# The order of weighing and scanning on VectorE in the last stage of a vision-tower kernel

## The chip, the cores and the metric

The kernel runs on one core of a Trainium2 chip. The metric is the device time of one execution in microseconds (us). A core has TensorE (PE), VectorE (DVE), ScalarE (ACT), GpSimd (POOL) and SyncE (SP). They run their own instruction streams in order and meet only at semaphores.

## What is computed

A tokenizer (two attention blocks over image patches), then one layer: a state-space scan and a mixture of experts. The program has three stages; only the third, which holds the scan and the experts, is touched. Its scan is this part of the reference, with 16 states (N) for each of 768 channels (D), 4 images, 3136 tokens:

```python
delta = jax.nn.softplus(x @ W_D + b_D + p_Delta)
dA = delta[..., None] * A
A_bar = jnp.exp(dA)
B_bar = (A_bar - A) / dA * delta[..., None] * Bproj[:, :, None, :]

def step(h, inp):
    a, b, c, xl = inp
    h = a * h + b * xl[..., None]
    y = jnp.einsum('bn,bdn->bd', c, h)
    return (h, y)
```

## The kernel before

The third stage is the function `tail`. Tokens are cut into 28 units of 448 (UNITS, T). A unit has 24 steps (STEPS); a step k takes 128 channels times four of the 16 states, laid out as four groups g = 0 to 3 of 128 rows and 448 tokens. Groups 0 and 1 are the first pair, 2 and 3 the second. `n` is the running number of a step, 672 in all. For each step:

- POOL `weigh_in` (L1622) writes x times B into a slot of the ring `v`, six slots; two steps later `weigh_out` (L1634) multiplies the scanned slot by C.
- ACT `step` (L1928) writes the decays, exp(A times delta), of a pair into PSUM (`decay(g)`), two instructions a pair. Each pair has one PSUM place, so the decays of a pair for step k wait until the scan of that pair for step k-1 is done (`free_pair`).
- DVE `weigh` (L2038) turns a group of the slot into (decay - A) times v. It waits for both decays of its pair, by the semaphore `s_a`.
- DVE `scan` (L2047) runs the recurrence over both groups of a pair at once, 901 elements long. It waits for the weighings of its pair (`s_wt`), and for the first pair also for the start states, which ACT writes (`start_states`, L1899).
- ACT `keep_states` (L1889) copies the last states of all four groups when both scans are done. POOL's `weigh_out` waits for it.
- PE `step` (L1734) sums over the states after POOL's `weigh_out`.

ACT's order within step k is: start states of k, decays of the first pair of k, then other work due at k, then the states kept of k-1, then decays of the second pair of k, then other work due at k + 0.5. The other work belongs to the neighbouring units: projection, normalisation and delta of the unit ahead (`front`), the experts of the unit behind (`mlp`). Constants such as A_GL = 17 or V_OH = 13 say at which step it stands. Step 17 holds most of ACT's: two table loads, four Gelu (L1952), three Relu (L1873). On DVE the other work stands behind step k: L2090 (one expert product, at 12, 14, 15 and 16), L2121 (the mask, two at 17 and two at 18), L2028 (delta, at 18 and 19) and small ones. PE makes the products that L2090 and L2121 take (L1665, L1785).

OWN is empty, so `own_scan` is never taken.

Of the kernel before, what the change touches and what calls it, by code (L numbers as in the profile page):

```python
# [1281 lines left out]
OWN = ()  # L1282
# [4 lines left out]
def others(n):  # L1287

    i, k = divmod(n, STEPS)
    return i * (STEPS - len(OWN)) + sum(j not in OWN for j in range(k + 1))  # L1290

def owned(n):

    return n + 1 - others(n)

def tail(nc, sem, w, c, t2, w1c, xd, dd, bcd, out):

    with ExitStack() as ctx:  # L1300
# [10 lines left out]
        def decay(g):  # L1311

            at = g // 2 * 1024 + g % 2 * GW
            return flat[:, at + 2:at + T + 2]

        def decays(pair):
            row = flat[:, 1024 * pair:1024 * pair + 2 * GW]
            return row.rearrange("p (g t) -> p g t", g=2)[:, :, 2:T + 2]
# [685 lines left out]
        def _(dve):  # L2004
# [26 lines left out]
            def weigh(i, k, g):  # L2031

                n = STEPS * i + k
                if g == 0:
                    dve.wait_ge(s_v, n + 1)
                dve.wait_ge(s_a, 4 * n + g // 2 * 2 + 2)
                row = v[:, n % RING, g, 2:T + 2]
                stt(row, decay(g), aa[:, 4 * k + g:4 * k + g + 1], row, ALU.subtract, ALU.mult).then_inc(s_wt, 1)  # L2038

            def scan(i, k, pair):  # L2040

                n = STEPS * i + k
                row = v[:, n % RING, 2 * pair:2 * pair + 2, :].rearrange("p g t -> p (g t)")[:, 1:GW + T + 2]
                if pair == 0:
                    dve.wait_ge(s_s0, others(n))
                dve.wait_ge(s_wt, 4 * n + 2 * pair + 2)
                nc.vector.tensor_tensor_scan(row, flat[:, 1024 * pair + 1:1024 * pair + GW + T + 2], row, 0.0, ALU.mult,  # L2047
                                             ALU.add).then_inc(s_sc, 1)

            def own_scan(i, k, pair):  # L2050

                n = STEPS * i + k
                first = i % J3 == 0
                if not first:
                    dve.wait_ge(s_sv, 2 * owned(n - STEPS) + pair - 1)
                for g in range(2 * pair, 2 * pair + 2):
                    dve.wait_ge(s_wt, 4 * n + g + 1)
                    nc.vector.tensor_tensor_scan(decay(g), decay(g), v[:, n % RING, g, 2:T + 2],
                                                 0.0 if first else st[:, 4 * k + g:4 * k + g + 1], ALU.mult,
                                                 ALU.add).then_inc(s_sp, 1)  # L2060
                if k // Q == 0 and pair == 0:
                    dve.wait_ge(s_lc[k % Q], 16 * (i + 1))
                dve.wait_ge(s_sp, 4 * owned(n) + 2 * pair - 2)
                tt(v[:, n % RING, 2 * pair:2 * pair + 2, 2:T + 2], decays(pair),
                   ct[:, k % Q:k % Q + 1, :].to_broadcast([128, 2, T]), ALU.mult).then_inc(s_cv, 1)

            def step(i, k):
                for pair in range(2):
                    weigh(i, k, 2 * pair)
                    weigh(i, k, 2 * pair + 1)  # L2070
                    if k in OWN:
                        own_scan(i, k, pair)
                    else:
                        scan(i, k, pair)

            def mlp(i, k):
                if k == V_VAR:
# [80 lines left out]
            for i in range(UNITS + 1):  # L2158
                for k in range(TAIL if i == UNITS else STEPS):
                    if i < UNITS:  # L2160
                        step(i, k)
                    if i >= 2 and k + STEPS < TAIL:
                        mlp(i - 2, k + STEPS)
                    if i >= 1:
                        mlp(i - 1, k)
                    if i + 1 < UNITS:
                        front(i + 1, k)
# [156 lines left out]
```

## Time and profile before

| | us |
|---|---|
| median of 3 runs | 8267.98 |
| lowest, highest | 8265.39, 8268.63 |
| the profiled execution | 8263.06 |
| its span on the core | 8261.3 |
| of it from the first L2038 to the last scan | 4935 |

The span is what the trace covers; the 1.8 us around it are launch and end. The profiled execution stands 4.9 us below the median. The page gives the busy time of each engine, the trace single instructions with the idle time ahead of each and what ended it.

### The profile page before, as it was taken

To read this page: it belongs to the slowest core of one execution; us is meant where nothing else is said; L and a number is where in the kernel's file an instruction comes from. 1 tells how busy PE (TensorE), PEld (TensorE's weight loads), DVE (VectorE), ACT (ScalarE), POOL (GpSimd) and SP (SyncE) were. 2 spreads that over 40 slices of the span, in tenths; PEclk is the share of its full clock that TensorE was granted. 3 is DMA by queue.
4 is the path that set the end of the run, shared out by engine and by line. 5 is a ranking of instruction groups with operands and counts; after the bars stand their busy time and mean duration, and the time that the engine had idled before them with its cause. 6 is when DMAs were issued, how large, how long until landed. Compare 5 with 4: busy or idle time off the path is not lost.

```text
span 8261.3 us, 86870 instructions
## 1 busy us (share of the span) xinstructions
PE 7327.8 (89%) x31004; PEld 2931.6 (35%) x31004; DVE 6205.4 (75%) x6573; ACT 4337.3 (53%) x7781; POOL 5547.7 (67%) x2487
## 2 busy tenths in 40 slices
PE   8999999869999975688888888888888888888987
PEld 6444444324444421133333333333333333333323
DVE  2566666742333345999999999999999999999995
ACT  3666666753444433555555555555555555555552
POOL 0111111148766614989999889999889998889994
PEclk9999999989999987789999889998989998988988
DMA  1111111135554413233333333333333333333331
GB/s 40 34 47 42 46 43 38 45 77 114 102 103 100 102 34 107 93 124 120 120 110 116 114 124 120 120 110 116 111 128 120 120 110 116 110 126 122 121 107 54
DMA packets 358648, 786.32 MB, mean 95 GB/s; under 512 B 72229, under 2 KB 284726, under 8 KB 350728
## 3 DMA queue, kind: packets, MB, share of 16 engines
q1 hardware_dynamic: 322168, 690.47, 28.4%
q0 software_dynamic: 21712, 51.75, 2.5%
q10 hardware_dynamic: 14336, 38.54, 1.3%
q8 instruction: 246, 4.03, 0.2%
q14 instruction: 186, 1.52, 0.1%
HBM read 597.06 MB, written 183.35 MB: 94 GB/s over the span
## 4 chain that ended last, share of the span: by engine, by line
DVE 28%; PE 15%; issue 11%; POOL 4%; ACT 4%; DMA 0%; DVEq 0%; SPq 0%; ACTq 0%; POOLq 0%
DVE v L2038 13%; DVE v L2047 13%; PE ps L1665 3%; POOL v L1634 3%; PE ps L1670 2%; PE ps L1672 2%; PE ps L1734 2%; PE ps L1679 2%; POOL v L1622 1%; DVE dl L2028 1%; PE ps L1681 1%; PE ps L1785 1%; ACT ps L1928 1%; ACT gm L1952 1%; PE ps L1798 0%
## 5 line engine op out<-in xcount | busy, mean ns | idle before, releaser
L2047 DVE TENSOR_TENSOR_SCAN v<-ps,v 128x901 f32<-128x901 f32 x1344 | 2732.1, 2033 | 95.0 <-DVE v L2038 2.7
L1634 POOL TENSOR_TENSOR v<-v,ct 128x1792 f32<-128x1792 f32 x672 | 2257.6, 3360 | 479.0 <-ACT st L1889 477.8
L1622 POOL TENSOR_TENSOR v<-xr,bt 128x1792 f32<-128x1792 f32 x672 | 2258.1, 3360 | 82.3 <-DMA xr<-h_by_channel 82.3
L1928 ACT ACTIVATE ps<-dr,aa 128x448 f32<-128x448 f32 x2688 | 1595.9, 626 | 1319.6 <-DVE v L2047 1303.2
L2038 DVE SCALAR_TENSOR_TENSOR v<-ps,aa,v 128x448 f32<-128x448 f32 x2688 | 1687.5, 669 | 71.5 <-ACT ps L1928 67.9
L1734 PE MATMUL ps<-v,dg 128*32 128x448 f32 x5376 | 792.3, 632 | 616.2 <-POOL v L1634 395.1
L236 POOL DMA_DIRECT2D tokens<-ob x448 | 235.3, 532 | 1529.9 <-DVE ob L563 1486.9
L1798 PE MATMUL ps<-w_or_w,gm 128*112 128x384 f32 x1792 | 694.4, 535 | 3.0 <-DMA w_or_w<-in_w 3.0
L1665 PE MATMUL ps<-h,w_or_w 128*128 128x448 f32 x1344 | 588.7, 592 | 84.9 <-DVE bcs L2022 84.9
L1889 ACT ACTIVATE st<-v 128x4 f32<-128x4 f32 x672 | 140.9, 210 | 893.5 <-DVE v L2047 893.5
L1670 PE MATMUL ps<-x,wpa 128*128 128x448 f32 x1008 | 497.1, 632 | 7.6 <-DVE w_or_w L2154 6.9
L1734 PEld LDWEIGHTS ps<-v,dg 128*32 128x32 f32 x5376 | 126.3, 114 | 1026.3 <-POOL v L1634 550.2
L1798 PEld LDWEIGHTS ps<-w_or_w,gm 128*112 128x112 f32 x1792 | 338.6, 197 | 386.9 <-issue 174.4
L1672 PE MATMUL ps<-x,wpb 64*128 64x448 f32 x1008 | 452.2, 580 | 0.0
L929 PE MATMUL ps<-xt,wa 128*64 128x448 f32 x2016 | 435.1, 565 | 0.0
L552 DVE COPY ht<-ps 112x512 f32<-112x512 f32 x112 | 77.4, 691 | 464.8 <-ACT kp L433 464.8
L1665 PEld LDWEIGHTS ps<-h,w_or_w 128*128 128x128 f32 x1344 | 268.4, 206 | 408.3 <-issue 302.6
L586 DVE RECIPROCAL qpn<-qpn 128x448 f32<-128x448 f32 x112 | 330.7, 2953 | 3.9
L1238 DVE TENSOR_TENSOR kq<-ps,rsa 128x896 f32<-128x896 f32 x56 | 61.1, 1091 | 358.4 <-PE ps L937 337.5
L1670 PEld LDWEIGHTS ps<-x,wpa 128*128 128x128 f32 x1008 | 202.0, 210 | 260.3 <-issue 257.8
L290 PE MATMUL ps<-wki,h 128*112 128x256 f32 x896 | 275.9, 389 | 1.9 <-DVE hu L544 1.9
L1672 PEld LDWEIGHTS ps<-x,wpb 64*128 64x128 f32 x1008 | 175.8, 187 | 275.1 <-issue 275.1
(328 smaller groups left out, 11558.6 us busy)
## 6 DMA issues: line engine op xcount, KB each, us to landing
xr<-h_by_channel SPq DMA_DIRECT2D x168, 896.0 KB, 4.9
dr<-delta_by_channel SPq DMA_DIRECT2D x168, 896.0 KB, 4.7
x<-tokens SPq DMA_DIRECT2D x252, 224.0 KB, 5.3
tokens<-ob POOLq DMA_DIRECT2D x448, 112.0 KB, 2.4
w_or_w<-in_w SPq DMA_DIRECT2D x29, 1536.0 KB, 6.4
w_or_w<-centred_w SPq DMA_DIRECT2D x27, 1536.0 KB, 9.0
h_by_channel<-h SPq DMA_DIRECT2D x112, 336.0 KB, 4.8
delta_by_channel<-dl SPq DMA_DIRECT2D x224, 168.0 KB, 2.8
```

Source lines behind the costliest of these rows:

```text
L586: nc.vector.reciprocal(qpn[:, u % 3, :], qpn[:, u % 3, :]).then_inc(s_dr, 1)
L929: mm(ps[half[g], o, 0:T], wa[:, j, cols], xt[:, 2 * (n % 3) + g, 0:TR2, j:j + 2 * S2 - 1:2], start=(j == 0), stop=False)
L1622: tt(v[:, n % RING, :, 2:T + 2], xr[:, dc % 2, :].rearrange("p (i t) -> p i t", i=4), bt[:, q:q + 1, :].to_broadcast([128, 4, T]), ALU.mul ...
L1634: tt(v[:, n % RING, :, 2:T + 2], v[:, n % RING, :, 2:T + 2], ct[:, q:q + 1, :].to_broadcast([128, 4, T]), ALU.mult).then_inc(s_cm, 1)
L1665: last = mm(into, weights(dc), h[:, i % 3, dc, :], start=(dc == 0), stop=(dc == DC - 1))
L1670: mm(into, even(j), x3[:, 0:TR3, j:j + 2 * S3 - 1:2], start=(j == 0), stop=False)
L1672: return mm(into, odd(j - 3), x3[0:64, 1:TR3 + 1, j - 3:j - 4 + 2 * S3:2], start=False, stop=(j == 5))
L1734: last = mm(ps[32 * g:32 * g + 32, YB, 0:T], dg[:, 4 * k + g, :], v[:, n % RING, g, 2:T + 2], start=(q == 0), stop=False)
L1798: mm(into[:, 0:D // 2], gm[:, m, cs], w2[:, m, lo:lo + D // 2], start=(m == 0), stop=False)
L1928: fn(decay(g), dr[:, dc % 2, g, :], ACT.Exp, scale=aa[:, 4 * k + g:4 * k + g + 1]).then_inc(s_a, 1)
L2038: stt(row, decay(g), aa[:, 4 * k + g:4 * k + g + 1], row, ALU.subtract, ALU.mult).then_inc(s_wt, 1)
L2047: nc.vector.tensor_tensor_scan(row, flat[:, 1024 * pair + 1:1024 * pair + GW + T + 2], row, 0.0, ALU.mult, ALU.add).then_inc(s_sc, 1)
```

## The change

On DVE, `step` weighs groups 0, 1 and 2, scans the first pair, weighs group 3 and scans the second pair. Before it weighed 0 and 1, scanned, weighed 2 and 3, and scanned. The instructions are the same ones, and each keeps its waits. The branch to `own_scan` goes, and with OWN empty nothing goes with it. Behind the edit line numbers fall by two (L2090 and L2121 become L2088 and L2119).

```diff
             def step(i, k):
-                for pair in range(2):
-                    weigh(i, k, 2 * pair)
-                    weigh(i, k, 2 * pair + 1)
-                    if k in OWN:
-                        own_scan(i, k, pair)
-                    else:
-                        scan(i, k, pair)
+                for g in range(3):
+                    weigh(i, k, g)
+                scan(i, k, 0)
+                weigh(i, k, 3)
+                scan(i, k, 1)
```

DVE around step 17 (from the last L2090 to the first L2028), before. The scan prints as SCALAR_TENSOR_TENSOR with 901 elements.

```order
L2090 TENSOR_TENSOR gm<-ps,rs2t 128x448
L2038 SCALAR_TENSOR_TENSOR v<-ps,aa,v 128x448 x2
L2047 SCALAR_TENSOR_TENSOR v<-ps,v 128x901
L2038 SCALAR_TENSOR_TENSOR v<-ps,aa,v 128x448 x2
L2047 SCALAR_TENSOR_TENSOR v<-ps,v 128x901
L2121 TENSOR_TENSOR gm<-gm,ps 128x448 x2
```

The same place in the changed kernel:

```order
L2088 TENSOR_TENSOR gm<-ps,rs2t 128x448
L2038 SCALAR_TENSOR_TENSOR v<-ps,aa,v 128x448 x3
L2047 SCALAR_TENSOR_TENSOR v<-ps,v 128x901
L2038 SCALAR_TENSOR_TENSOR v<-ps,aa,v 128x448
L2047 SCALAR_TENSOR_TENSOR v<-ps,v 128x901
L2119 TENSOR_TENSOR gm<-gm,ps 128x448 x2
```

The third weighing stands ahead of the first scan, in this step as in all 672. The other engines' streams are the same in both. ACT around step 17, from the decays of the first pair of step 17 to the decays of the second pair of step 18:

```order
L1928 ACTIVATE ps<-dr,aa 128x448 x2
L1952 ACT_TABLE_LOAD
L1952 ACTIVATE gm<-gm,b 128x448 x4
L1953 ACT_TABLE_LOAD
L1873 ACTIVATE dl<-ps,pc 128x448 x3
L1889 ACTIVATE st<-v 128x4
L1928 ACTIVATE ps<-dr,aa 128x448 x2
L1873 ACTIVATE dl<-ps,pc 128x448 x3
L1899 ACTIVATE v<-st 128x4
L1928 ACTIVATE ps<-dr,aa 128x448 x2
L1917 ACTIVATE h<-ps 128x448
L1878 ACTIVATE dl<-dl,small 128x1344
```

The second L1928 here holds the decays for which the third and fourth weighings of step 17 wait, the third L1928 those of the first pair of step 18, which follow the first scan of step 17.

## Rows read from the trace of the kernel before

**Rows 1.** Stretches: us, then each engine's busy us (and instructions), clock, DMA.

```profile
3221.00:8156.00 4935.00, 4237.14 (x15031) 1557.72 (x15032) 4674.94 (x4815) 2615.80 (x5542) 4457.14 (x1341) 0.89 0.35 115
```

**Rows 2.** Groups by line, 5600 to 7200: busy us, mean ns; idle before, releasers.

```profile
L2047 DVE TENSOR_TENSOR_SCAN v<-ps,v 128x901 f32<-128x901 f32 x434 | 882.2, 2033 | 30.8 <-ACT v L1899 0.9 <-DVE v L2038 0.5
L2038 DVE SCALAR_TENSOR_TENSOR v<-ps,aa,v 128x448 f32<-128x448 f32 x867 | 544.4, 669 | 19.0 <-ACT ps L1928 17.8
L1928 ACT ACTIVATE ps<-dr,aa 128x448 f32<-128x448 f32 x868 | 515.4, 626 | 425.1 <-DVE v L2047 425.1
```

**Rows 3.** Timeline, DVE, a step without other work: start us, us, instruction.

```profile
6020.90 1.25 DVE L2038 SCALAR_TENSOR_TENSOR v<-ps,aa,v 128x448 f32<-128x448 f32 x2
6022.25 2.03 DVE L2047 TENSOR_TENSOR_SCAN v<-ps,v 128x901 f32<-128x901 f32 x1
6024.20 1.25 DVE L2038 SCALAR_TENSOR_TENSOR v<-ps,aa,v 128x448 f32<-128x448 f32 x2
6025.49 2.03 DVE L2047 TENSOR_TENSOR_SCAN v<-ps,v 128x901 f32<-128x901 f32 x1
6027.44 1.25 DVE L2038 SCALAR_TENSOR_TENSOR v<-ps,aa,v 128x448 f32<-128x448 f32 x2
```

**Rows 4.** Timeline, ACT, the same step.

```profile
6021.02 0.21 ACT L1889 ACTIVATE st<-v 128x4 f32<-128x4 f32 x1 [2.04 <-DVE v L2047]
6021.13 1.18 ACT L1928 ACTIVATE ps<-dr,aa 128x448 f32<-128x448 f32 x2
...
6024.32 1.20 ACT L1928 ACTIVATE ps<-dr,aa 128x448 f32<-128x448 f32 x2 [1.88 <-DVE v L2047]
```

**Rows 5.** Timeline, ACT, step 1 of a unit.

```profile
6045.44 1.50 ACT L1843 ACTIVATE sq<-h 128x448 f32<-128x448 f32 x3
6047.17 0.21 ACT L1889 ACTIVATE st<-v 128x4 f32<-128x4 f32 x1 [0.23 <-DVE v L2047]
```

**Rows 6.** Timeline, DVE, other work ahead of step 8, step 12 and step 15.

```profile
6092.95 0.62 DVE L2079 TENSOR_TENSOR rs2t<-ps,rs2t 32x448 f32<-32x448 f32 x1
...
6121.13 1.26 DVE L2038 SCALAR_TENSOR_TENSOR v<-ps,aa,v 128x448 f32<-128x448 f32 x2
...
6143.66 0.62 DVE L2090 TENSOR_TENSOR gm<-ps,rs2t 128x448 f32<-128x448 f32 x1 [0.53 <-PE ps L1665]
```

**Rows 7.** Timeline, ACT, the decays of the second pair of step 12.

```profile
6121.96 1.20 ACT L1928 ACTIVATE ps<-dr,aa 128x448 f32<-128x448 f32 x2
```

**Rows 8.** Timeline, all engines, steps 17 and 18.

```profile
6164.52 0.21 ACT L1889 ACTIVATE st<-v 128x4 f32<-128x4 f32 x1
6164.62 1.20 ACT L1928 ACTIVATE ps<-dr,aa 128x448 f32<-128x448 f32 x2
6164.81 3.36 POOL L1634 TENSOR_TENSOR v<-v,ct 128x1792 f32<-128x1792 f32 x1 [6.97 <-ACT st L1889]
...
6165.85 1.28 DVE L2038 SCALAR_TENSOR_TENSOR v<-ps,aa,v 128x448 f32<-128x448 f32 x2 [2.03 <-ACT ps L1928]
...
6168.50 0.56 ACT L1917 ACTIVATE h<-ps 128x448 f32<-128x448 f32 x1
6168.92 1.44 ACT L1878 ACTIVATE dl<-dl,small 128x1344 f32<-128x1344 f32 x1
...
6170.24 0.22 ACT L1889 ACTIVATE st<-v 128x4 f32<-128x4 f32 x1
...
6171.45 3.36 POOL L1634 TENSOR_TENSOR v<-v,ct 128x1792 f32<-128x1792 f32 x1
...
6174.86 1.72 PE L1734 MATMUL ps<-v,dg 128*32 128x448 f32 x8 [4.03 <-POOL v L1634]
...
6178.48 0.62 DVE L2121 TENSOR_TENSOR gm<-gm,ps 128x448 f32<-128x448 f32 x1 [1.69 <-PE ps L1785]
```

**Rows 9.** Waits of DVE from 3400 on: us in total, times, longest.

```profile
DVE gm L2121 <- PE ps L1785: 70.1, 58, 2.0
...
DVE gm L2090 <- PE ps L1665: 48.6, 51, 5.6
```

## The prediction

> **What bounds the kernel now.** I read the stretches first. From the first weighing to the last scan DVE is busy for 4675 of 4935 us, 95%; POOL 90%, PE 86%, ACT 53% [rows 1]. So in this stage DVE sets the pace, and time added to its chain is time added to the kernel unless a wait of DVE swallows it. The groups by line say what it does: scans of 2.03 us and weighings of 0.67 [rows 2]. ACT's decays show 425 us of idle time ahead of them, all ended by DVE's scans: ACT is quick but lives on what DVE frees. So a loop runs through both: scan, decays, weighing, scan. The question is how much slack that loop has, and the timeline of a plain step answers it.
>
> **A plain step before** [rows 3]. With the first weighing's start as 0, the first scan starts at 1.35, the third weighing 1.95 later (3.30), the second scan at 4.59, the next step at 6.54. Two weighings span 1.25 us at 0.67 each, so the second starts 0.58 behind the first: neighbours without a wait between them overlap. The scan starts only behind the end of the weighing it needs: 0.10 after it for the first pair (1.35 against 1.25), 0.04 for the second (1.29 against 1.25).
>
> The decays of the second pair [rows 4]: the previous second scan ends, ACT keeps the states at 6021.02, starts the two decays at 6021.13 and is done at 6022.31, 1.41 after the first weighing of the step. DVE sees that 0.03 later (6164.62 + 1.20 = 6165.82, weighing at 6165.85 [rows 8]), so they are usable at **1.44**. The old third weighing came at 3.30: slack 1.86.
>
> **The same step after.** Nothing is added or removed; one weighing moves ahead of one scan. It would start at 2 x 0.58 = 1.16, and has to wait until 1.44: a new wait of 0.28. Queued behind it on DVE are both scans and the fourth weighing, and behind the first scan ACT's next decays. From there: scan 0.60 behind it (1.28 for two at 6165.85, after an idle moment, less 0.67 is 0.61 [rows 8]; 0.58 otherwise), at 2.04. Its own inputs were done at 1.25, so the bubble ahead of this scan goes. Fourth weighing 1.95 later, 3.99. It alone takes about 0.66, the second scan starts 0.04 behind: 4.69. Next step 6.64. So a plain step goes from 6.54 to 6.64, **+0.10**.
>
> Where the decays are early enough, the step is 1.16 + 0.58 + 1.95 + 0.70 + 1.95 = 6.34, **-0.20**. That is so where DVE has other work between the second scan and the next first weighing (0.62 us in L2079, say [rows 6]), which gives ACT the 0.28.
>
> Neither price is in the trace, since no third weighing stands ahead of a scan. Bounds: the follow-on of the scan behind an unrelated instruction is between 0.50 and 0.67, and the single weighing with its scan between 0.66 and 0.74; that makes a plain step +0.0 to +0.2.
>
> **One unit of 24 steps**, added up:
>
> - 13 plain steps (0 to 7, 9, 11, 21 to 23): 13 x 0.10 = +1.3.
> - Step 1. ACT's other work there leaves 0.23 us before it keeps the states [rows 5]. From first to second scan DVE now takes 1.95 + 0.70 = 2.65 in place of 1.95 + 1.29 = 3.24, 0.59 less, so ACT is late by 0.59 - 0.23: +0.36. At the other plain steps ACT has 0.85 or more there and hides it.
> - Step 12. The decays are done at 6121.96 + 1.20 = 6123.16 and usable at 6123.19 [rows 7]; the third weighing would start at 6121.13 + 1.16 = 6122.29 [rows 6]. Wait 0.90, less the 0.20: +0.7. The old order hid it behind the first scan.
> - Steps 8, 10, 15, 19, 20 have cover: 5 x -0.20 = -1.0.
> - Steps 13 and 14 have cover too, but L2090 behind step 14 waits 0.53 us for PE now [rows 6], and PE's products follow POOL, which follows the scans of step 12. The 0.4 won becomes a longer wait: 0.
> - Steps 16 to 18. The first scan of step 16 comes 0.40 later within its step (0.58 for the weighing put ahead of it, less the bubble of 0.18). ACT's decays for step 17 wait for it, then the table loads, Gelu and Relu, then the states kept and the second decays: all +0.40, and the DVE wait of 2.03 at 6165.85 with them [rows 8]. At that place the new order has a whole scan more behind the wait, some 1.9 us that used to lie in front. Is it on the path? What ends last there is the chain by which the mask product reaches L2121: states kept of step 17, POOL L1634 at 6171.45, PE at 6174.86, L2121 at 6178.48, before which DVE idles 1.69 [rows 8]. After, without the 0.40: first scan 6166.45 to 6168.48, decays of step 18 to 6169.65, L1917 and L1878 (0.42 and 1.32 from start to next start) to 6171.4, states kept then, POOL 0.29 later at 6171.7 in place of 6171.45. DVE itself gets to L2121 at about 6178.5. So +0.25, and with the 0.40 **+0.65**; 1.2 us of the 1.9 go into the old wait. The gain of step 16 is lost, since the chain leaves from its first scan.
>
> Sum: 1.3 + 0.36 + 0.7 - 1.0 + 0 + 0.65 = **+2.0 us a unit**, 28 units: +56 us. The profiled execution would go from 8263 to 8319, the median from 8268 to **8324**.
>
> SyncE, POOL and PE issue the same streams; no DMA moves. POOL needs 2 x 3.36 = 6.72 a step, more than a plain step of 6.54, but made up for at each unit's waits; a slower DVE only eases that.
>
> The trace shows that DVE neighbours overlap unless one waits for the other (1.25 for two weighings of 0.67 [rows 3]), which is what the new order uses. 
>
> **The rivals.**
>
> 1. *The bubble stays* (that rule as a mechanism): the scan starts as far behind the unrelated third weighing as it did behind its own second. Then covered steps gain nothing, plain ones lose the full 0.28: 13 x 0.28 + 0.36 + 0.9 + 0.65 = 5.5 a unit, +155, 8423. Against: 1.25 is less than 2 x 0.67, and scan to weighing is 1.95 at a length of 2.03 [rows 3]. Chance 0.05.
> 2. *Step 17 is exposed.* The scan behind the Gelu wait lands on the path: +1.95 in place of 0.65, 1.3 x 28 = +36, 8360. It decides at L2121: my working has DVE arrive only 0.2 us ahead of PE. Chance 0.15.
> 3. *The old waits swallow it.* DVE waits for PE 70.1 + 48.6 us in this stage [rows 9], 4 us a unit, twice what I add. If PE's products came at times of their own, the delay would vanish: 8268 to 8285. Against: PE waits for POOL, and POOL for states kept behind the scans, so they move along. Chance 0.13.
> 4. *Faster: the bubble outweighs the wait.* The price of a plain step is the wait less 0.18; the unit breaks even at 2.0 / 13 = 0.15 below my +0.10, at a wait of 0.13 us in place of 0.28. With no wait at all it is 13 x -0.20 for 13 x 0.10, -1.9 a unit, 8215. For: 0.28 is a difference of numbers near 1.4. Against: it begins with the end of the previous scan and ACT's order is fixed. Chance 0.07.
>
> **How the numbers follow.** My forecast has 0.60. 0.2% is 16.5 us, about what a measurement of this kernel can tell from no change. Slower: forecast, rivals 1 and 2, 0.80. Same: rival 3, 0.13. Faster: rival 4, 0.07. Range: 8324 with +-0.07 for a plain step is +-25; rival 2 takes the top to 8365; the upper part of rival 3 the bottom to 8278. Rivals 1, 4 and half of 3 stay outside, 0.19.
>
> **What would show it.** Plain steps of 6.64 us, with L2038 in a form of three, then one, and an idle time of some 0.3 us inside the three, released by ACT L1928; in all L2038 should wait for it some 13 x 0.28 x 28 = 100 us more from plain steps, 25 from step 12, 10 from step 1. No idle time ahead of the first scan. The wait of L2121 for PE falls from 1.69 to about 0.5 at its first. The 2.03 ahead of the third weighing of step 17 becomes about 4. I am wrong if plain steps measure under 6.5 or over 6.75, or if L2121's waits don't shrink.

## The result

| us | before | changed |
|---|---|---|
| median of 5 runs | 8267.98 | 8299.93 |
| lowest, highest | 8265.39, 8271.39 | 8298.85, 8301.81 |
| span of the profiled execution | 8261.3 | 8298.1 |

The changed kernel takes 1.0039 times as long, 95% interval 1.0024 to 1.0054. That is 32 us more; the prediction was 56 us more, 8324, with a range of 8278 to 8365, and "slower" at 0.80. The direction, the mechanism and most prices held. The sum was 24 us too high.

The stage's stretch, answering [rows 1] (us; then PE, PE loads, DVE, ACT, POOL busy us and instructions; clock; DMA share; GB/s), and the groups by line, answering [rows 2]:

```profile
3223.00:8191.00 4968.00, 4230.90 (x15027) 1551.32 (x15028) 4649.46 (x4815) 2623.37 (x5542) 4461.68 (x1341) 0.89 0.35 114
```

```profile
L2047 DVE TENSOR_TENSOR_SCAN v<-ps,v 128x901 f32<-128x901 f32 x432 | 876.1, 2028 | 7.5
L2038 DVE SCALAR_TENSOR_TENSOR v<-ps,aa,v 128x448 f32<-128x448 f32 x863 | 554.2, 671 | 73.7 <-ACT ps L1928 72.5
L1928 ACT ACTIVATE ps<-dr,aa 128x448 f32<-128x448 f32 x864 | 512.9, 625 | 533.1 <-DVE v L2047 532.9
```

The stage is 33 us longer, while DVE's busy time fell by 25 us. The idle time ahead of the scans went from 30.8 to 7.5 us in these 1600 us: that is the bubble. The idle time ahead of the weighings went from 19.0 to 73.7, nearly all of it ended by ACT's decays: that is the new wait. Both things that the change does are in these two differences, and the second, 55 us, is larger than the first, 23 us. Some 23 of the 55 us are no loss, though: these 1600 us hold nine units, and in each the wait at step 17 grew by 2.5 us, most of which the waits for the mask products gave back, as the rows of steps 17 and 18 below show.

A plain step of DVE in the changed kernel, from the timeline, answering [rows 3]:

```profile
6062.82 1.25 DVE L2038 SCALAR_TENSOR_TENSOR v<-ps,aa,v 128x448 f32<-128x448 f32 x2
6064.26 0.68 DVE L2038 SCALAR_TENSOR_TENSOR v<-ps,aa,v 128x448 f32<-128x448 f32 x1 [0.19 <-ACT ps L1928]
6064.86 2.02 DVE L2047 TENSOR_TENSOR_SCAN v<-ps,v 128x901 f32<-128x901 f32 x1
6066.80 0.66 DVE L2038 SCALAR_TENSOR_TENSOR v<-ps,aa,v 128x448 f32<-128x448 f32 x1
6067.50 2.03 DVE L2047 TENSOR_TENSOR_SCAN v<-ps,v 128x901 f32<-128x901 f32 x1
6069.45 1.25 DVE L2038 SCALAR_TENSOR_TENSOR v<-ps,aa,v 128x448 f32<-128x448 f32 x2
```

From 6062.82 the third weighing starts at 1.44, the first scan at 2.04, the fourth weighing at 3.98, the second scan at 4.68, the next step at 6.63. The prediction had 1.44, 2.04, 3.99, 4.69 and 6.64. The wait reads 0.19 and not 0.28 because the profile counts idle time from the end of the second weighing (0.67 long), and the third would have started 0.09 before that end.

ACT around the same step, answering [rows 4]:

```profile
6062.94 0.21 ACT L1889 ACTIVATE st<-v 128x4 f32<-128x4 f32 x1 [0.98 <-DVE v L2047]
6063.05 1.18 ACT L1928 ACTIVATE ps<-dr,aa 128x448 f32<-128x448 f32 x2
...
6066.92 1.19 ACT L1928 ACTIVATE ps<-dr,aa 128x448 f32<-128x448 f32 x2 [2.56 <-DVE v L2047]
```

The decays of the second pair end at 6064.23 and the weighing starts at 6064.26. ACT starts the copy as soon as the previous scan is done. So this step is a closed loop without slack: second scan, copy, decays, third weighing, first scan, fourth weighing, second scan.

Steps 17 and 18, answering [rows 8], all engines:

```profile
6188.56 1.20 ACT L1928 ACTIVATE ps<-dr,aa 128x448 f32<-128x448 f32 x2
...
6189.79 0.68 DVE L2038 SCALAR_TENSOR_TENSOR v<-ps,aa,v 128x448 f32<-128x448 f32 x1 [4.75 <-ACT ps L1928]
...
6195.62 3.36 POOL L1634 TENSOR_TENSOR v<-v,ct 128x1792 f32<-128x1792 f32 x1 [0.17 <-ACT st L1889]
...
6199.03 1.72 PE L1734 MATMUL ps<-v,dg 128*32 128x448 f32 x8 [3.15 <-POOL v L1634]
...
6202.64 0.62 DVE L2119 TENSOR_TENSOR gm<-gm,ps 128x448 f32<-128x448 f32 x1 [0.18 <-PE ps L1785]
```

DVE idles 4.75 us ahead of the third weighing of step 17, where it idled 2.03 (the prediction had about 4), and 0.18 us ahead of the third mask product, where it idled 1.69. So the scan that now stands behind the long wait goes mostly into the old wait, as worked out.

DVE's waits from 3400 on, answering [rows 9]:

```profile
DVE v L2038 <- ACT ps L1928: 214.2, 404, 4.8
DVE gm L2088 <- PE ps L1665: 51.6, 39, 5.9
DVE gm L2119 <- PE ps L1785: 28.6, 55, 0.9
```

The wait for the decays was 51.5 us before, all of it at step 17. Now step 17 has 120 us of it, the 12 plain steps other than step 1 have 62, step 12 has 21 and step 1 has 11. The prediction had 100, 25 and 10 for the last three; the 100 is too high because it counts 0.28 a step where the profile, as above, shows 0.19.

**The ledger.** The trace gives the start of each first weighing, so the length of each of the 24 steps. The table has the mean over the 26 units between the first and the last, changed kernel less before, beside the prediction, in us a unit:

| steps | predicted | measured |
|---|---|---|
| 0 to 7, 9, 11, 21 to 23 (step 1 among them) | +1.66 | +1.36 |
| 8, 10, 15, 19, 20 | -1.0 | -1.03 |
| 12 | +0.7 | +0.38 |
| 13, 14 | 0 | -0.05 |
| 16 to 18 | +0.65 | +0.53 |
| sum | +2.0 | +1.19 |

1.19 x 28 is 33 us. Of the +0.38 at step 12, 0.13 is one single wait of 3.3 us in the second unit, ahead of L2088 for a product of TensorE; no other unit of this trace has one over 0.2 us there.

### The profile page after: what moved, and what is told of

Its sections match the earlier page's. It is cut to its first block, busy times and chain, and to the rows that moved or that the text cites. A ratio compares the mean times of both kernels' runs of the same rounds, so it can differ in the third digit from the quotient of the medians.

```text
span 8298.1 us, 86870 instructions
## 1 busy us (share of the span) xinstructions
PE 7325.2 (88%) x31004; PEld 2926.6 (35%) x31004; DVE 6180.9 (74%) x6573; ACT 4345.5 (52%) x7781; POOL 5552.9 (67%) x2487
## 4 chain that ended last, share of the span: by engine, by line
DVE 30%; PE 11%; ACT 9%; issue 8%; POOL 4%; DMA 0%; SPq 0%; DVEq 0%; ACTq 0%; POOLq 0%
DVE v L2047 21%; ACT ps L1928 6%; DVE v L2038 5%; POOL v L1634 3%; PE ps L1665 2%; PE ps L1672 2%; POOL v L1622 1%; PE ps L1679 1%; DVE dl L2028 1%; PE ps L1734 1%; PE ps L1785 1%; PE ps L1670 1%; PE ps L1681 1%; ACT gm L1952 1%; PE ps L1798 1%
## 5 line engine op out<-in xcount | busy, mean ns | idle before, releaser
L1928 ACT ACTIVATE ps<-dr,aa 128x448 f32<-128x448 f32 x2688 | 1595.6, 625 | 1677.7 <-DVE v L2047 1660.8
L2038 DVE SCALAR_TENSOR_TENSOR v<-ps,aa,v 128x448 f32<-128x448 f32 x2688 | 1726.2, 671 | 238.1 <-ACT ps L1928 234.5
L1798 PE MATMUL ps<-w_or_w,gm 128*112 128x384 f32 x1792 | 722.1, 552 | 2.9 <-DMA w_or_w<-in_w 2.9
L1670 PE MATMUL ps<-x,wpa 128*128 128x448 f32 x1008 | 477.0, 611 | 7.1 <-DVE w_or_w L2152 6.4
```

Source lines behind the costliest of these rows:

```text
L1670: mm(into, even(j), x3[:, 0:TR3, j:j + 2 * S3 - 1:2], start=(j == 0), stop=False)
L1798: mm(into[:, 0:D // 2], gm[:, m, cs], w2[:, m, lo:lo + D // 2], start=(m == 0), stop=False)
L1928: fn(decay(g), dr[:, dc % 2, g, :], ACT.Exp, scale=aa[:, 4 * k + g:4 * k + g + 1]).then_inc(s_a, 1)
```

## The experiments

Each is an edit to the changed kernel: to the list of steps with the new order, to one other place, or, in four of them, to more than one place. Times are medians; the ledgers are of the one profiled execution. Where only some steps have the new order, `step` reads like this:

```diff
-                for g in range(3):
+                late = k in (8, 10, 13, 14, 15, 19, 20)
+                for g in range(3 if late else 2):
                     weigh(i, k, g)
                 scan(i, k, 0)
-                weigh(i, k, 3)
+                for g in range(3 if late else 2, 4):
+                    weigh(i, k, g)
                 scan(i, k, 1)
```

### The new order where it has cover (`k in (8, 10, 13, 14, 15, 19, 20)`)

> The new order in steps 8, 10, 13, 14, 15, 19 and 20 alone, where other work on VectorE stands ahead of the first weighing; the old order in the other 17. Theory (a scan behind an unrelated weighing saves a bubble of 0.20 us, and the price of the change lies in the plain steps): each of these steps 0.20 us shorter, what is won in 8, 10, 13 and 14 partly lost again in L2090's waits for PE behind steps 12 and 14, so 0.6 to 1.0 us a unit, 17 to 28 us in all, 8240 to 8251. Rival (the bubble is no property of the order, the times only shift): 8268, within 5.

Measured: 8234.0 us, ratio to before 0.9957 (0.9944 to 0.9969), 34 us less than before. The theory holds, and more was won than it allowed. The ledger against before: -0.20 in each of 8, 10, 13, 15, 19 and 20; step 14 +0.17, in place of -0.20. Steps 12 and 16, which keep the old order, came out 0.16 and 0.20 shorter, because L2090 waits less behind them than before (behind step 12 0.26 a unit in place of 0.39, behind step 16 nothing in place of 0.17); why it does is open. So 10 us of the gain were not won in the seven steps themselves. What steps 13 and 14 won went into L2090 behind step 14, which waits 0.89 a unit in place of 0.55. DVE's waits from 3400 to 8100:

```profile
DVE gm L2121 <- PE ps L1785: 68.8, 54, 2.0
DVE v L2038 <- ACT ps L1928: 53.5, 28, 2.0
DVE gm L2090 <- PE ps L1665: 32.2, 36, 1.0
```

In the same stretch the kernel before has 66.4, 51.0 and 31.2. The wait for the decays stands at step 17 alone, as before, so none of the seven steps meets the new wait. The total at L2090 is nearly the same, but it moved: less behind steps 12 and 16, more behind step 14.

### The new order in plain steps alone (`k < 8 or k in (9, 11) or k > 20`)

> The new order in the 13 plain steps alone (0 to 7, 9, 11, 21 to 23). Theory (a plain step costs 0.09 us, step 1 costs 0.34, and nothing behind takes it back): 12 x 0.09 + 0.34 = 1.4 us a unit, +40 us, 8308. Rival (part of what is lost ahead of step 12 goes into L2090's waits for PE, 0.4 us a unit on average behind step 12 in the kernel before): 0.9 to 1.0 a unit, +26, 8294.

Measured: 8289.4 us, ratio 1.0025 (1.0015 to 1.0035): +21, and the rival is right, the theory wrong. The plain steps cost what they should (+0.09 each, step 1 +0.33, together +1.36), but step 12 is 0.44 us shorter than before although nothing in it is changed. The reason stands behind it. In the kernel before, an L2090 of step 12, unit 20:

```profile
6833.41 2.03 DVE L2047 TENSOR_TENSOR_SCAN v<-ps,v 128x901 f32<-128x901 f32 x1
6836.18 0.62 DVE L2090 TENSOR_TENSOR gm<-ps,rs2t 128x448 f32<-128x448 f32 x1 [0.73 <-PE ps L1665]
```

The same place in this run:

```profile
6850.86 2.03 DVE L2047 TENSOR_TENSOR_SCAN v<-ps,v 128x901 f32<-128x901 f32 x1
6852.81 0.60 DVE L2090 TENSOR_TENSOR gm<-ps,rs2t 128x448 f32<-128x448 f32 x1
```

DVE comes later, the product of TensorE doesn't, and the wait is gone. Counted from the first weighing of its unit, step 12 starts at 80.6 us before and at 81.75 here, while the product is done at 86.4 to 88.3 before and at 87.5 here in 22 of 26 units. Before, this wait was there in 17 of 27 units, at 0.28 to 0.77 us, and missing in the others; the prediction read step 12 in the unit at 6121, which is one without.

### The old order in step 12 (`k != 12`)

> The new order in all steps but 12. Theory (the 0.7 us that step 12 costs fits into L2090's wait behind it in most units): as the changed kernel, 8295 to 8300. Rival (the prediction's working, step 12 costs 0.7 us a unit on the path): 19 us less, 8281.

Measured: 8279.7 us, ratio 1.0012 (1.0004 to 1.0021), 20 less than the changed kernel. The rival is right, and here the rival was the prediction's own working: step 12 does cost 0.7 us a unit. The theory that L2090's wait swallows it was mistaken in one point: the wait can be used once only, and the delay of the plain steps has used it by then. Step 12 is 0.35 shorter than before in this run and 0.38 longer in the changed kernel, 0.73 between them. The single wait of 3.3 us is 0.13 of that. In units without any wait at L2090 step 12 takes 8.03 us in the old order and 8.72 in the new one: the price itself is 0.69.

### The old order in steps 16 and 17, and in 17 alone

> The new order in all steps but 16 and 17. Theory (steps 16 to 18 together cost 0.6 us a unit, because the first scan of 16, from which ScalarE's long piece starts, comes 0.4 later, and the mask products 0.25 later still): 17 us less than the changed kernel, 8283. Rival (the first scan of 17, put behind a wait of some 4.7 us, is wholly exposed, and step 18 is short for another reason): 28 x 1.9 = 53 us less, 8247.

> The new order in all steps but 17. Theory (of the 20 us that steps 16 and 17 cost together, most is the first scan of step 16 coming 0.4 us later, from which ScalarE's decays, table loads and Gelu start; step 17 adds 0.25 at the mask products): 4 to 7 us less than the changed kernel, 8293 to 8296. Rival (the 20 us are step 17's scan behind the long wait): 8280.

Measured: 8280.3 us (1.0014, 1.0005 to 1.0023) with both old, 8288.5 us (1.0024, 1.0014 to 1.0035) with 17 old. The lengths of steps 16, 17 and 18 together:

| | us |
|---|---|
| before | 29.10 |
| changed | 29.62 |
| 17 old | 29.39 |
| 16 and 17 old | 28.99 |

So step 17 brings 0.23 (the prediction had 0.25) and step 16's later first scan 0.40 (0.40). The rival of an exposed scan falls: of the 2.3 us by which step 17 is longer in the changed kernel, step 18 gives back 1.7. The 8288 is 5 us under what was expected. By the ledger steps 16 to 18 give the 6 us that were expected and step 12 another 4, of which 3.3 are the single wait in the second unit of the changed kernel's trace, which this run's trace doesn't have. Whether the executions without a trace have that wait is not known.

### One more small copy in ScalarE's path

```diff
                 act.wait_ge(s_sc, 2 * others(n))
+                after(act, s_du, others(n) - 1)
+                fn(small[:, 7:8], v[:, n % RING, 0, T + 1:T + 2], ACT.Copy).then_inc(s_du, 1)
                 fn(st[:, 4 * k:4 * k + 4], v[:, n % RING, :, T + 1], ACT.Copy).then_inc(s_st, 1)
```

> The changed kernel with one more small copy on ScalarE (one column, into a spare one) ahead of each copy that keeps the states, so that it lies between the second scan and the next decays. Theory (a plain step is a closed loop of second scan, copy, two decays, third weighing, first scan, fourth weighing, second scan): the 0.11 us between two such starts goes into every plain step, 6.63 to 6.74, and into steps 1 and 12; some 15 x 0.11 = 1.65 us a unit, +46, 8345. Rival (ScalarE is only 53% busy and the 0.19 us wait of a plain step is a fixed cost of a semaphore): plain steps stay at 6.63, 8300.

Measured: 8338.4 us, ratio 1.0087 (1.0073 to 1.0100), 38 more than the changed kernel. Plain steps measure 6.72, and the wait in them is 0.28 in place of 0.19 (here the weighing is L2041, the scan L2050):

```profile
6068.49 1.25 DVE L2041 SCALAR_TENSOR_TENSOR v<-ps,aa,v 128x448 f32<-128x448 f32 x2
6070.02 0.69 DVE L2041 SCALAR_TENSOR_TENSOR v<-ps,aa,v 128x448 f32<-128x448 f32 x1 [0.29 <-ACT ps L1931]
```

```profile
6068.61 0.20 ACT L1891 ACTIVATE small<-v 128x1 f32<-128x1 f32 x1 [0.61 <-DVE v L2050]
6068.72 0.19 ACT L1892 ACTIVATE st<-v 128x4 f32<-128x4 f32 x1
6068.81 1.18 ACT L1931 ACTIVATE ps<-dr,aa 128x448 f32<-128x448 f32 x2
```

The second copy starts 0.11 us behind the first and the decays 0.09 behind that, where they used to start 0.11 behind the only copy: the decays come 0.09 later and so does the step. ACT is busy for half of the time, and yet a delay of 0.09 us in its part of the loop costs 0.09 us a step. The loop theory holds.

### The copy behind the decays

```diff
+                    if i < UNITS:
+                        step(i, k, 1)
                     if i >= 1 and k == 0:
                         keep_states(i - 1, STEPS - 1)
                     elif i < UNITS and k > 0:
                         keep_states(i, k - 1)
-                    if i < UNITS:
-                        step(i, k, 1)
```

> The changed kernel with the copy that keeps the states behind the second pair's decays in place of ahead of them, in every step. Theory (closed loop): plain steps lose the copy's 0.11 us, 6.63 to 6.52, just under the 6.54 of before; but the states are kept 1.1 us later, and where GpSimd and TensorE lead to the mask products of step 18 that comes on top: -15 x 0.11 + 1.1 = -0.5 us a unit, 8286. Rival (GpSimd has room everywhere, nobody waits for the kept states): -1.65 a unit, 8254.

Measured: 8283.6 us, ratio 1.0021 (1.0011 to 1.0030). Plain steps measure 6.53: the loop is 0.10 shorter, and the change no longer costs anything there. Step 18 is 1.1 us longer than in the changed kernel (11.53 against 10.42), because POOL gets the kept states later and the mask product moves with them; L2119 waits 1.27 us again:

```profile
6194.48 0.62 DVE L2119 TENSOR_TENSOR gm<-gm,ps 128x448 f32<-128x448 f32 x1 [1.27 <-PE ps L1785]
```

Again the same edit does two different things: in a plain step nobody waits for the kept states, and behind step 17 the mask product does, by way of POOL and PE. The 8283.6 is what the theory has (8286); its rival with 8254 falls. With the copy behind the decays in plain steps alone, and the old order in 12, 16 and 17 (so the new one in 18 too):

> The new order in all steps but 12, 16 and 17, and the copy that keeps the states behind the decays in the 13 plain steps. Theory: plain steps 0.02 us shorter than before, step 1 0.2 longer, the covered ones as in the run with the new order there alone, -1.3 us a unit: 8230 to 8236, no better than that run. Rival (the later copy in plain steps holds up GpSimd): over 8245.

Measured: 8228.7 us, ratio 0.9956 (0.9943 to 0.9968). As the theory has it, no better than the covered steps alone (8234) by more than the runs spread. Plain steps 6.53, step 1 still 6.77. The ledger shows why nothing more comes of it: step 12 is 0.34 shorter than in that run, since nothing waits at the expert product behind it any more, and step 16 is 0.58 longer, since the product behind it now waits 0.5 a unit. What is won at one wait for TensorE is met again at the next.

### Where the gain of steps 13 and 14 goes

L2090 behind step 14 waits 0.55 us a unit before and 0.87 in the changed kernel. The changed kernel's rows show what sets that product's time. Behind step 12 DVE writes `eq` (L2108, L2110 in the kernel before), TensorE turns it (L1773), and from there to the end of the product no matmul of it waits for another engine:

```profile
6152.79 0.19 DVE L2108 TENSOR_TENSOR eq<-ps,sm 112x32 f32<-112x32 f32 x1
6153.03 0.94 PE L1773 MATMUL ps<-ident,eq 112*9 112x112 f32 x8 [1.07 <-DVE eq L2108]
...
6162.59 4.78 PE L1665 MATMUL ps<-h,w_or_w 128*128 128x448 f32 x12
...
6167.40 0.63 DVE L2088 TENSOR_TENSOR gm<-ps,rs2t 128x448 f32<-128x448 f32 x1 [0.93 <-PE ps L1665]
```

From the end of `eq` to the start of this L2088 it is 14.42 us; in the kernel before, and in every run that takes the product behind step 14, the median is 14.4 to 14.5. So whatever delays step 12 delays the product, and whatever shortens steps 13 and 14 only lengthens the wait. In the next three runs DVE takes that product behind step 15:

```diff
-        V_VAR, V_ENC, V_IN, V_LOG, V_EQ, V_OH, V_MASK = 7, 9, (12, 14, 15, 16), 11, 12, 13, (17, 17, 18, 18)
+        V_VAR, V_ENC, V_IN, V_LOG, V_EQ, V_OH, V_MASK = 7, 9, (12, 15, 15, 16), 11, 12, 13, (17, 17, 18, 18)
```

> The old order in every step, and the second expert product taken behind step 15. Tells how much of the last two runs is the later read alone. Theory: the kernel before waits 0.57 us a unit there, so -16 us, 8251, and the new order in covered steps is worth the other 38. Rival (the later read alone gives most of it): under 8235.

> The new order in steps 8, 10, 13, 14, 15, 19 and 20 alone (first of these runs: 8234), and VectorE takes the second expert product behind step 15 in place of behind step 14, where it waits 0.9 us for TensorE there. Theory (the product comes at a time that VectorE's order doesn't move, so what steps 13 and 14 win is given back at L2090): the wait goes and is not found again behind step 15, up to 0.9 us a unit, 8209 to 8215. Rival (TensorE is held up behind the later read and the wait only moves): 8230 to 8240.

> The same later read; the new order in all steps but 1, 12, 16 and 17; in the 12 plain steps left the copy that keeps the states stands behind the decays. Theory: as the run before it, less 12 x 0.02 us a unit, 6 us: 8203 to 8210, the best of all. Rival (the later copies or the later read hold up GpSimd and TensorE): 8225 or more.

Measured: 8240.0 us with the old order (0.9966, 0.9954 to 0.9978), 8213.0 us with the new order in covered steps (0.9936, 0.9923 to 0.9948), 8198.5 us with the last mix (0.9918, 0.9905 to 0.9932). The 8213 is what its theory has. The 8240 lies between its theory (8251) and its rival (under 8235): the later read alone is worth 27 us, 11 more than the 0.57 us wait it removes. By the ledger steps 14 and 15 are together 0.72 a unit shorter, 20 us, and step 16 is 0.20 shorter, 6 us: L2090 behind it waited in four units before, 4.7 us in all, and waits in none here. The run with the new order in covered steps has the same 0.20 without the later read, so those 6 us are not surely the read's. The new order in covered steps adds 27, the new order in plain steps with the later copy, without step 1, another 14, of which 7 were expected (12 x 0.02 x 28), so that the last run ends 5 us under its theory. The trace puts the 14 elsewhere than the theory did: 4 us are the plain steps, and 11 us are step 12, behind which L2090 waited 0.30 us a unit in the run at 8213 and doesn't wait in the last one; why the product is in time there is open. With the later read both L2090 stand together behind step 15 and neither waits (the run at 8213):

```profile
6125.08 1.13 DVE L2090 TENSOR_TENSOR gm<-ps,rs2t 128x448 f32<-128x448 f32 x2
```

The last kernel is the fastest: 69 us under before, 0.8%. Its stage takes 4868 us where it took 4935 [rows 1]:

```profile
3223.00:8091.00 4868.00, 4156.65 (x15022) 1519.53 (x15026) 4652.44 (x4814) 2614.96 (x5543) 4455.62 (x1342) 0.90 0.36 117
```

Not tried: a third weighing that waits for its own decay only, which is there 0.56 us earlier (an estimate: two decays take 1.18, one 0.63). The kernel lays the decays of a pair side by side, across its PSUM banks of 512 columns, so DVE would read a bank while ACT writes it; no run shows what that does.

## Why the prediction was right, and where not

**DVE sets the pace: held.** The change moved only DVE instructions, and the time of every plain step moved with them. The other half of the loop counts as much: 0.09 us of work added to ACT is 0.09 us in every plain step.

**The price of a plain step, +0.10: held, +0.09.** All five starts in it were within 0.01 us. The follow-on of the scan behind an unrelated weighing, which no row of before showed, is 0.60 (6064.26 to 6064.86), inside the bounds of 0.50 to 0.67; the single weighing with its scan is 0.70 (6066.80 to 6067.50), inside 0.66 to 0.74. What decided between 6.54 and 6.64 was not an average of busy times but one row of ACT set against one row of DVE.

**The covered steps, -0.20: held to 0.01,** in the changed kernel and alone.

**Step 1, +0.46 (0.36 and the 0.10): +0.33.** The overrun of ACT was sized from idle time; but where ACT's own work ends late, the copy behind it starts before that work is done and not 0.03 us after a semaphore. Measured in the changed kernel, ACT, step 1:

```profile
6068.43 1.49 ACT L1843 ACTIVATE sq<-h 128x448 f32<-128x448 f32 x3
6069.83 0.19 ACT L1889 ACTIVATE st<-v 128x4 f32<-128x4 f32 x1
6069.93 1.18 ACT L1928 ACTIVATE ps<-dr,aa 128x448 f32<-128x448 f32 x2
```

The squares run to 6069.92, the copy starts at 6069.83. DVE waits 0.44 there, 0.25 more than in the other plain steps.

**Step 12, +0.7: the price held, the sum did not.** Leaving it out gave the 20 us that it was put at. The step of the prediction that failed is the unstated one ahead of it: that what the plain steps add reaches step 12 in full. L2090's wait for TensorE behind step 12, 0.39 us a unit, takes part of it: with the new order in plain steps alone, step 12 came out 0.44 shorter. I took that place from one unit, which happened to have no such wait; the line's total, 48.6 us in 51 waits [rows 9], was in my rows, more than step 14's 0.53 x 28 = 15, and I did not ask where the rest was. It was 11 us behind step 12, 5 behind step 16, and 17 behind 8100 us, at the stage's end. By the ledger step 12 is 0.32 a unit under its term, 9 of the 24 us of the sum. It would be some 12 without the single wait of 3.3 us in this trace, so that wait brought the total nearer to my forecast by luck. Plain steps at 0.09 for 0.10 are 5, step 1 is 4, steps 16 to 18 are 3, steps 13 and 14 are 1.

**Steps 13 and 14, "the gain is lost": nearly held.** Measured -0.05 a unit, while the wait behind step 14 went from 0.55 to 0.87. The product does move with step 12, as I had it: in the changed kernel and in the run with step 12 old, where that step is 0.7 shorter, the wait behind step 14 is the same 0.9. The link is another one. I had it go by POOL; the rows show it go by `eq`, which DVE itself writes behind step 12.

**Steps 16 to 18, +0.65: held, +0.53.** The two runs give 0.40 and 0.23, as worked out; the 0.10 between their sum and the 0.53 is step 16, which even in the old order is 0.15 shorter in the run with 16 and 17 old than before, with less wait at L2090 behind it. DVE reached the mask product 0.18 us ahead of TensorE, where I had 0.2. The wait there fell from 1.69 to 0.18, further than the 0.5 I named, and the idle time ahead of the third weighing of step 17 became 4.75, where my own terms give 2.03 + 1.95 + 0.40 = 4.4 and I wrote about 4.

**The rivals.** *The bubble stays*: refuted by [rows 3] already and now by the 0.60. The section of the Trainium skill that I set it on (VectorE: DVE Perf Modes, "The DRAIN you can't avoid") also has a sentence that I left out, that a next instruction which isn't held starts earlier; the trace agrees with that one, with 0.60 between a weighing of 0.68 and the scan behind it. *Step 17 is exposed*: refuted, 0.23. *The old waits swallow it*: partly right, and this is what my forecast lacked. The wait behind step 12 took 0.4 us a unit. The 1.5 a unit that the mask products' waits took was in my sum already, as the 1.2 of steps 16 to 18. *Faster*: came true with the new order in the covered steps alone (8234); the copy behind the decays in every step was not enough for it (8284).

## What to carry to other kernels

An instruction moved ahead of another loses the cover that the other gave it: before moving it, set the end of what it waits for against its new start, in one plain period, from the rows of both engines. Where the same loop has periods with cover and periods without, price and place them apart; here the same edit is worth -34 us in seven of the 24 steps, +21 in thirteen, and +20 each in step 12 and in 16 and 17 together. These don't add up to the +32 of all at once, because they share the waits at L2090. A wait further on takes up a delay once, and only in the iterations in which it exists, so read it in several iterations and not in one.

## What the runs showed that I had not expected

A wait of 0.57 us a unit, at one L2090, was worth about as much as the order of weighing and scanning in its best steps: taking one product a step later saved 27 us. And the granted clock of TensorE differed a little between the profiled executions (0.917 in the changed kernel, 0.928 in the fastest one); whether that moves the waits at L2090 stays open.
